# Second half of a hybrid block: queries, two mixtures of experts and attention in one program of numbered steps

## Chip, core, metric

One core of one Trainium2 chip runs the program. The metric is the device time of one launch in microseconds, as a median of several runs. Everything is computed in float32 precision. Engines are named as the profile names them: PE (TensorE), DVE (VectorE), ACT (ScalarE), POOL (GpSimd), SP (SyncE, which only issues transfers here).

## What is computed

The input x has 4 batches of 512 tokens of 128 numbers (16 tiles of 128 tokens). Cut to what matters:

```python
x = x + attn_a(layernorm(x))   # two test-time-training steps, then the queries through the trained weights
x = x + ffn(layernorm(x))      # mixture of experts
x = x + attn_b(layernorm(x))   # block-causal attention, 16 heads of 64, over 512 tokens
x = x + ffn(layernorm(x))      # the same mixture again
# attn_a ends:  h = swish(q @ gate) * (q @ val);  o = h @ proj @ proj_w + proj_b
# ffn:  gates = softmax(x @ Wg + bg);  the best 2 of 8, scaled to sum 1
#       out = sum over the chosen two of (x @ We[e] + be[e]) * gate
```

All 8 experts are computed for every token, and six of the eight weights are zero.

## The kernel before

The program has phases, each a block of its own with a barrier of all engines behind it. Up to the queries (projections, two rounds of gradients and of orthogonalisation) nothing changes but the table of biases below.

*Products.* A product that needs float32 precision is three matmuls (`mm3`, L100 to L102): both operands are split in a high part and the rest, and the rests' product is left out.

*Queries* (`query_phase`). Per batch of 512 tokens, four chunks of hidden units: two `mm3` (gate into q_G_, value into q_U_), sigmoid on ACT (L860), two products on DVE (L913, L919). Four output tiles of a batch (L890, 128x128 matmuls against the folded weight) stand between the chunks of the next. DVE adds them to x (L924) and takes statistics (L160).

*Mixture* (`moe_phase`, called twice). For all 16 tiles at once: mean and variance from the statistics (`ln_vector`, seven small DVE operations, a square root on ACT, a reciprocal). Per batch DVE normalises four tiles (L1095), PE transposes them (L1047), ACT and DVE split them (L1025, L1101), PE computes the scores of the experts (twelve matmuls with 8 columns). When all scores are there, one chain of small DVE operations on 128x128 values (L1112 to L1134) finds the two best experts of every token and their weights. PE turns the weights and multiplies them with a table that has the experts' biases at the places of all 16 tiles, and DVE adds that to x (L1140). Then, tile by tile, PE computes eight experts into two banks of PSUM; ACT scales three of them (L1037), POOL adds these up (L1014, L1016), DVE scales and adds the other five (L1158), POOL adds the two sums into x (L1005).

*Attention* (`attention_phase`). 32 pairs of heads, in each three groups of query tiles (tile 3; tile 2; tiles 1 and 0), so 96 steps. In step s PE computes the scores of group s, transposes the weights of group s-3, and projects the next queries (first step of a pair), keys (second) or values (third); in every third step it also multiplies a whole pair's weights with the values (L1409). DVE takes scores with mask and row minimum (L1484), copies transposed weights, keys, values (L1495, L1471, L1476), ACT does exponentials (L1325) and other copies, POOL scales rows (L1295). A step of the first group is called heavy below: it holds L1409's forty records; the steps of the second and third group are light. Eight banks of PSUM: three for scores (`psS`), two for transposed weights (`psT`), one for outputs of the heads (`psO`), two that projections and outputs take in turn (`psP`): a use waits until the use two places earlier is read.

Each engine runs its instructions in the order written in its loop and waits for semaphores of the others.

## Time and profile before

| | |
|---|---|
| median of 3 runs | 867.99 us (867.47 to 868.44) |
| the profiled execution's own time | 866.14 us |
| its span in the profile | 863.7 us |
| PE busy | 774.2 us (90%) |
| DVE busy | 545.4 us (63%) |
| ACT busy | 394.9 us (46%) |
| POOL busy | 270.7 us (31%) |
| chip clock granted to PE, mean | 0.94 |

The span is that of the profiled execution from its first to its last instruction; its own time includes 2.4 us around it. Busy times of engines overlap. PE runs at one of two clocks, 1.2 or 2.4 GHz; a granted clock of 0.50 in a stretch is the lower one. In timelines a row's "x6" merges six records of a kind; a 128x128 float32 matmul that isn't a transpose leaves two records, so L1419's 32 matmuls are x64.

### The profile page before, as it was taken

How to read it: one execution, taken by the hardware profiler on the slowest of the kernel's cores; microseconds unless marked ns; L12 is line 12 of the kernel's file. 1: busy time of each engine (PE TensorE's matmuls, PEld its weight loads, DVE VectorE, ACT ScalarE, POOL GpSimd, SP SyncE). 2: the span in 40 equal slices, each digit the busy share in tenths (PEclk: the TensorE clock that was granted, in tenths of full speed). 3: DMA queues.
4: the chain of work that ended last, by engine and by line, in shares of the span. 5: the costliest groups of instructions: out<-in, count | busy, mean ns of one | idle time of the engine just before them, and what ended most of it. 6: DMA issues, size and time to landing. Idle time of an engine off the chain costs nothing. (4 is left out here: it accounts for less than half of the span.)

```text
span 863.7 us, 15529 instructions
## 1 busy us (share of the span) xinstructions
PE 774.2 (90%) x5512; PEld 616.6 (71%) x5512; DVE 545.4 (63%) x1649; ACT 394.9 (46%) x1118; POOL 270.7 (31%) x476
## 2 busy tenths in 40 slices
PE   3669999897999988987858999999999999999786
PEld 1239999775999976677645677777777777777765
DVE  3945656444555535664796776776677666665468
ACT  4733333243333234312255766565556555564224
POOL 4830000002445002100372444343334333333027
PEclk9969999997999999895898999999999999999678
DMA  3040000000000000000000000000000000000001
GB/s 104 1 134 1 1 2 1 1 1 1 1 1 2 1 1 1 0 1 1 0 2 0 2 2 2 2 2 1 2 2 1 2 2 2 2 1 2 1 0 50
DMA packets 9466, 7.17 MB, mean 8 GB/s; under 512 B 1584, under 2 KB 9008, under 8 KB 9264
## 3 DMA queue, kind: packets, MB, share of 16 engines
q1 hardware_dynamic: 9392, 6.19, 2.3%
...
q14 instruction: 28, 0.23, 0.1%
...
## 5 line engine op out<-in xcount | busy, mean ns | idle before, releaser
L1295 POOL TENSOR_SCALAR t_p_<-t_p_,t_rinv_ 128x128 f32<-128x128 f32 (+3 forms) x256 | 132.1, 532 | 202.3 <-DVE t_rinv_ L1491 202.3
L1325 ACT ACTIVATE t_p_<-t_p_,t_nmin_ 128x128 f32<-128x128 f32 (+3 forms) x256 | 140.0, 551 | 9.1 <-DVE t_nmin_ L1484 9.1
L1484 DVE CUSTOM_DVE_ANT_0 t_p_<-t_S_,t_mask_ 128x128 f32<-128x128 f32 (+3 forms) x256 | 112.8, 487 | 21.7 <-PE t_S_ L1382 17.3
L1330 ACT ACTIVATE t_pT_<-t_T_ 128x384 f32<-128x384 f32 (+1 forms) x96 | 50.5, 526 | 118.3 <-PE t_T_ L1394 118.3
L1394 PEld LDWEIGHTS t_T_<-ident,t_p_ 128*128 128x128 f32 x640 | 68.2, 141 | 44.9 <-issue 26.0
L1382 PE MATMUL t_S_<-t_k_,t_q_ 64*128 64x256 f32 (+3 forms) x512 | 95.0, 468 | 0.1
L1394 PE MATMUL t_T_<-ident,t_p_ 128*128 128x128 f32 x640 | 90.8, 281 | 0.3 <-ACT t_pT_ L1330 0.3
L1409 PEld LDWEIGHTS t_O_<-t_pT_,t_v_ 128*64 128x64 f32 x1280 | 69.2, 137 | 11.0 <-ACT t_pT_ L1330 10.5
L1409 PE MATMUL t_O_<-t_pT_,t_v_ 128*64 128x128 f32 x1280 | 76.9, 275 | 0.0
L522 DVE SCALAR_TENSOR_TENSOR g_sw<-g_th,g_G 128x512 f32<-128x512 f32 x32 | 22.0, 688 | 71.3 <-ACT g_slope L436 66.2
L1382 PEld LDWEIGHTS t_S_<-t_k_,t_q_ 64*128 64x128 f32 x512 | 41.5, 185 | 26.9 <-DVE t_nmin_ L1484 12.3
L1495 DVE COPY t_pT_<-t_T_ 128x384 f32<-128x384 f32 (+1 forms) x96 | 57.3, 597 | 1.4 <-PE t_T_ L1394 1.3
L408 POOL TENSOR_TENSOR g_kl<-qkT,g_kh 128x128 fp32r<-128x128 f32 x32 | 14.6, 457 | 138.0 <-ACT g_kh L427 138.0
L1500 DVE COPY t_oT_<-t_O_ 128x512 f32<-128x512 f32 x32 | 22.1, 691 | 54.8 <-PE t_O_ L1409 54.8
L1325 ACT ACTIVATION_READ_ACCUMULATOR t_p_<-t_p_,t_nmin_ 128x1 f32 x256 | 48.6, 190 | 0.0
L440 ACT ACTIVATE g_hT<-g_H 128x512 f32<-128x512 f32 x32 | 19.1, 597 | 60.0 <-PE g_H L472 60.0
L1037 ACT ACTIVATE m_y_<-m_A_,m_wt_ 128x128 f32<-128x128 f32 x96 | 28.0, 367 | 25.4 <-PE m_A_ L102 25.4
L646 POOL TENSOR_TENSOR gvl<-gv,gvh 128x512 fp32r<-128x512 f32 x4 | 5.0, 1273 | 104.3 <-ACT gvh L751 104.3
L479 PEld LDWEIGHTS g_PT<-proj,g_hT 128*128 128x128 f32 x256 | 33.8, 193 | 2.6
L498 PE MATMUL acc<-qkv,g_dg 128*128 128x128 f32 x256 | 34.0, 276 | 1.0 <-DVE g_dg L549 1.0
L479 PE MATMUL g_PT<-proj,g_hT 128*128 128x128 f32 x256 | 34.1, 276 | 0.0
L498 PE MATMUL acc<-qkv,g_du 128*128 128x128 f32 x256 | 33.8, 275 | 0.0
(259 smaller groups left out, 1794.5 us busy)
## 6 DMA issues: line engine op xcount, KB each, us to landing
...
```

What stands on the lines that cost most here:

```text
L479: last = pe.matmul(pred, hT[:, t.ring, n * P:n * P + P], self.proj[:, n, :], start=(n == 0), stop=(n == NC - 1))
L498: last = pe.matmul(self.acc[:, n, m, :], src[:, t.ring, m * P:m * P + P], d[:, t.ring, :] if n == 2 else k, start=False, stop=False, skip_ ...
L1037: last = act.activation(y[:, t % 4, tile_of(k)], experts_of(t, e), ACT.Copy, scale=weight(t, e))
L1295: last = pool.tensor_scalar(pr[:, G.par, h, cols], pr[:, G.par, h, cols], rinv[:, G.par, n:n + 1], 1.0, ALU.mult, ALU.mult)
L1325: act.activation(pr[:, G.par, h, cols], pr[:, G.par, h, cols], ACT.Exp, bias=nmin[:, G.par, n:n + 1], scale=-1.0, accum_out=rsum[:, G.par, ...
L1330: act.activation(pT[:, G.par, 0, G.blocks], psT[:, 0, 0:G.width], ACT.Copy).then_inc(t["eA"], 1)
L1382: last = pe.matmul(psS[:, (2 * G.n + h) % 3, at_:at_ + (qt + 1) * P], qp[d, G.par, qt * P:qt * P + P], kp[d, G.par, 0:(qt + 1) * P], start ...
L1394: last = pe.transpose(psT[:, h, k:k + P], pr[:, G.par, h, at_:at_ + P], ident[:, :])
L1409: last = pe.matmul(psO[d, qt * P:qt * P + P], v[:, G.b % 2, n, G.p * P + h * DH:G.p * P + h * DH + DH], pT[:, G.par, h, at_:at_ + P], star ...
L1484: dve.tensor_tensor_reduce(pr[:, G.par, h, cols], psS[:, (2 * G.n + h) % 3, at_:at_ + keys], mask[:, SEQ - keys:SEQ], 1.0, -NEG, ALU.add, ...
L1495: dve.tensor_copy(pT[:, G.par, 1, G.blocks], psT[:, 1, 0:G.width]).then_inc(t["eB"], 1)
L1500: dve.tensor_copy(oT[:, b % 2, p, :], psO[:, :]).then_inc(t["oT"], 1)
```

## The change

Queries, both mixtures and the attention become one block, `second_half_phase`, without barriers. Its steps run from -38 to 116, and the attention's groups are steps 0 to 95 as before.

- The queries have steps -36 to -5, a chunk every second step, and the sixteen output products of a batch stand together in one step (-27, -19, -11, -3), in a bank of the scores.
- The two mixtures are eight *jobs*, one per batch: jobs 0 to 3 are the first mixture, 4 to 7 the second. `FRONT` is the step of a job's statistics; normalising, transposing, scores, top, three parts of the choice, weights and biases follow at +1 to +9. `EXPERTS` is the step of its first tile of experts; in the attention a tile's upper four experts (ACT scales all four, POOL sums) stand in one step and the lower four (DVE) in the next. Each job's chain works on 128x32 values instead of all tokens' 128x128.
- The standard deviation's inverse comes from a power of -0.5 on POOL, in place of ACT's root and DVE's reciprocal.
- psP has three banks, and the pair's outputs share them (`psO` is gone), as do all stages of the jobs: a use waits for the use three places earlier. Ten halves of tiles of jobs 6 and 7 use the five banks of scores and transposed weights once the attention is through with them.
- Each attention output tile is made in two halves of four heads' pairs. The last batch's first halves stand in steps 89 to 92, the second halves in step 101, with job 6's first experts.
- The biases' table has 32 rows instead of 128 and 512 columns instead of 2048, loaded by 4 transfers instead of 16.

```diff
-    LATE_LOADS = 10 + NT
+    LATE_LOADS = 10 + TPB
...
+    class Job:
+
+
+        FRONT = (-25, -17, 2, 20, 34, 58, 82, 102)
+        EXPERTS = (-16, -6, 11, 29, 43, 67, 101, 105)
...
+        def upper(self, n):
+
+            if self.closing == 1:
+                return self.first if n < 3 else self.front + 9
+            if self.closing == 0:
+                return self.first + (0, 1, 2, 4)[n]
+            return self.first + (n if self.j < 2 else 2 * n)
+
...
+        def summed(self, n):
+
+            if self.closing == 1:
+                return self.front + 9 + n
+            if self.closing == 0:
+                return self.first + (2, 3, 3, 5)[n]
+            return self.lower(n)
+
...
+            psG, psU, psO = psS[:, 0:2, :], psT, psS[:, 2, :]
...
+            QUERY = -36
+            ANSWER = 9
...
+            X_STEPS = [-9] + [IN_BATCH * b + 12 for b in range(BATCH - 1)]
+            OUT_STEPS = [IN_BATCH * b + step for b in range(BATCH)
+                         for step in (17, 18, 19, 20) + ((29, 30, 31, 32) if b < BATCH - 1 else (29, 29, 29, 29))]
...
+            halves = [("eh", 0), ("el", 0), ("eh", 1), ("el", 1), ("eh", 2)]
+            free = [psS[:, 0, :], psS[:, 1, :], psS[:, 2, :], psT[:, 0, :], psT[:, 1, :]]
+            spare = {(kind, j * TPB + n): bank_ for j in (NJ - 2, NJ - 1) for (kind, n), bank_ in zip(halves, free)}
...
+            emptied = {"q": (t["qe"], 1), "k": (t["ke"], 1), "v": (t["ve"], 1), "o": (t["res"], 1), "x": (t["xa"], 1),
+                       "pv": (t["oT"], 1), "mt": (m["l"], 1), "ml": (m["lg"], 1), "mw": (m["wl"], 1), "mb": (m["xb"], 1),
+                       "eh": (m["y"], 1), "el": (m["s"], 4)}
 
             def bank(kind, n):
-                return psP[:, place[kind, n] % 2, :]
+                return spare[kind, n] if (kind, n) in spare else psP[:, place[kind, n] % 3, :]
 
             def wait_bank(e, kind, n):
 
+                if (kind, n - TPB) in spare:
+                    sem, times = emptied[kind]
+                    e.wait_ge(sem, (n - TPB + 1) * times)
+                    return
+                if (kind, n) in spare:
+                    e.wait_ge(t["mx"], 8 * self.PAIRS)
+                    e.wait_ge(t["eA"], N)
+                    e.wait_ge(t["eB"], N)
+                    return
                 at_ = place[kind, n]
-                if at_ >= 2:
-                    before, m = uses[at_ - 2]
-                    e.wait_ge(emptied[before], m + 1)
+                if at_ >= 3:
+                    kind_, n_ = uses[at_ - 3]
+                    sem, times = emptied[kind_]
+                    e.wait_ge(sem, (n_ + 1) * times)
...
+                def power(kind, n, b):
+                    pool.wait_ge(t["var"], norm_of[kind, n] + 1)
+                    rows = slice(b * TPB, b * TPB + TPB)
+                    pool.tensor_tensor(self.rstd[:, rows], self.lnw[:, 3, rows], self.mhalf[:, rows], ALU.pow).then_inc(t["root"], 1)
+
+                def add_experts(J, n):
+                    i = J.j * TPB + n
+                    pool.wait_ge(m["y"], i + 1)
+                    if i:
+                        pool.wait_ge(m["z"], i)
+                    pool.tensor_tensor(half[:, :, :], y[:, i % 2, 0:2, :], y[:, i % 2, 2:4, :], ALU.add).then_inc(m["z0"], 1)
+                    pool.wait_ge(m["z0"], i + 1)
+                    if i > 1:
+                        pool.wait_ge(m["s"], 4 * (i - 2) + 2)
+                    pool.tensor_tensor(z[:, i % 2, :], half[:, 0, :], half[:, 1, :], ALU.add).then_inc(m["z"], 1)
+
+                def close(J, n):
+                    i = J.j * TPB + n
+                    pool.wait_ge(m["s"], 4 * i + 4)
+                    pool.tensor_tensor(x[:, J.b * TPB + n, :], a[:, i % 2, :], b_[:, i % 2, :], ALU.add).then_inc(m["x"], 1)
...
+                def output(b, half, n):
+                    i = (2 * b + half) * TPB + n
                     wait_bank(pe, "o", i)
-                    pe.wait_ge(t["oT"], (b + 1) * NP)
-                    for n in range(NP):
-                        last = pe.matmul(bank("o", i)[:, 0:P], oT[:, b % 2, n, m * P:m * P + P], wout[:, n, :],
-                                         start=(n == 0), stop=(n == NP - 1))
+                    pe.wait_ge(t["oT"], b * NP + half * TPB + TPB)
+                    for p in range(half * TPB, half * TPB + TPB):
...
+                def experts(J, n, kind, first, done):
+                    i = J.j * TPB + n
+                    cols = slice(first, first + 512)
+                    wait_bank(pe, kind, i)
+                    mm3(pe, bank(kind, i), mh[:, J.par, tile_of(n)], ml[:, J.par, tile_of(n)], weh[:, cols], wel[:, cols]).then_inc(done, 1)
...
+                for s in STEPS:
                     G, T, O = at(s, 0), at(s, LT), at(s, LV)
+                    if s == QUERY - 1:
+                        fold()
                     if G:
                         scores(G)
                     if T:
                         turn(T)
-                    if G:
...
+                def moments(b):
+                    st, rows = self.stats[:, b * TPB:b * TPB + TPB, :], slice(b * TPB, b * TPB + TPB)
+                    w = self.lnw[:, :, rows]
+                    taken.wait()
+                    chain(dve.tensor_tensor(w[:, 0, :], st[:, :, 1], st[:, :, 4], ALU.subtract))
+                    chain(dve.tensor_tensor(w[:, 1, :], w[:, 0, :], w[:, 0, :], ALU.mult))
+                    chain(dve.tensor_tensor(w[:, 2, :], st[:, :, 2], st[:, :, 5], ALU.add))
+                    chain(dve.scalar_tensor_tensor(w[:, 3, :], w[:, 1, :], P / 4.0, w[:, 2, :], ALU.mult, ALU.add))
...
+                def rank(J, src, high_, chosen):
+
+                    e_ = eq[:, J.par, :, :]
+                    g, h, k = src[:, J.par, :, :], high_[:, J.par, :], pm[:, J.par, :]
+                    link.next(dve.tensor_reduce(h, g, AX.X, ALU.max))
+                    link.wait()
+                    link.next(dve.tensor_tensor(e_, g, wide(h), ALU.is_equal))
+                    link.wait()
+                    link.next(dve.tensor_tensor(e_, e_, prio[:, :, :], ALU.mult))
+                    link.wait()
+                    link.next(dve.tensor_reduce(k, e_, AX.X, ALU.max))
+                    link.wait()
+                    link.next(dve.tensor_tensor(chosen[:, J.par, :, :], e_, wide(k), ALU.is_equal))
+
+                def route(J, part):
+                    r = J.par
+                    if part == 0:
+                        dve.wait_ge(m["prio"], 1)
+                        dve.wait_ge(m["e"], J.j + 1)
+                        link.wait()
+                        rank(J, gate, top1, sel)
+                    if part == 1:
+                        link.wait()
+                        link.next(dve.scalar_tensor_tensor(gate2[:, r, :, :], sel[:, r, :, :], -2.0, gate[:, r, :, :], ALU.mult, ALU.add))
+                        link.wait()
+                        rank(J, gate2, top2, sel2)
+                    if part == 2:
+                        link.wait()
+                        link.next(dve.tensor_tensor(tot[:, r, :], top1[:, r, :], top2[:, r, :], ALU.add))
+                        link.next(dve.tensor_tensor(sel[:, r, :, :], sel[:, r, :, :], sel2[:, r, :, :], ALU.add))
+                        link.wait()
+                        link.next(dve.tensor_tensor(sel[:, r, :, :], sel[:, r, :, :], gate[:, r, :, :], ALU.mult))
+                        link.next(dve.reciprocal(rtot[:, r, :], tot[:, r, :]))
+                        link.wait()
+                        dve.tensor_tensor(wt[:, r, :, :], sel[:, r, :, :], wide(rtot[:, r, :]), ALU.mult).then_inc(m["c"], 1)
+
...
+                def accumulate(J, n):
+                    i = J.j * TPB + n
+                    weight = lambda e: wt[:, J.par, n, e:e + 1]
+                    dve.wait_ge(m["c"], J.j + 1)
+                    dve.wait_ge(m["xb"], J.j + 1)
+                    dve.wait_ge(m["E"], i + 1)
+                    if i > 1:
+                        dve.wait_ge(m["x"], i - 1)
+                    for e in range(4):
+                        acc = (a, b_)[e % 2][:, i % 2, :]
+                        if e == 1:
+                            dve.wait_ge(m["z"], i + 1)
+                        if e > 1:
+                            dve.wait_ge(m["s"], 4 * i + e - 1)
+                        so_far = (x[:, J.b * TPB + n, :], z[:, i % 2, :])[e] if e < 2 else acc
+                        dve.scalar_tensor_tensor(acc, bank("el", i)[:, tile_of(e)], weight(e), so_far,
+                                                 ALU.mult, ALU.add).then_inc(m["s"], 1)
+
...
                     k.schulz_phase(step)
-            k.query_phase()
-        k.moe_phase(0)
-        k.attention_phase()
-        k.moe_phase(1)
+        k.second_half_phase()
```

Three places of the order show the moves. The first is on PE: the end of the queries before, and then a piece of the changed queries, from the third step with output products (m_A_ and t_P_ are banks that mixtures and projections use, q_O_ and t_S_ take the queries' outputs, t_T_ now also takes the value products).

```order
L100 MATMUL q_U_<-q_qh_,gvh 128x512
L101 MATMUL q_U_<-q_ql_,gvh 128x512
L102 MATMUL q_U_<-q_qh_,gvl 128x512
L890 MATMUL q_O_<-q_pw_,q_hT_ 128x128 x20
L829 UNCONDITIONAL_BRANCH
L1040 UNCONDITIONAL_BRANCH
L1047 MATMUL m_A_<-ident,m_xn_ 128x128 x8
L100 MATMUL m_A_<-wgh,m_xh_ 128x8
L101 MATMUL m_A_<-wgl,m_xh_ 128x8
```

```order
L1233 MATMUL t_S_<-t_pw_,t_oT_ 128x128 x16
L115 MATMUL t_S_<-t_xh_,gvh 128x512
L116 MATMUL t_S_<-t_xl_,gvh 128x512
L117 MATMUL t_S_<-t_xh_,gvl 128x512
L115 MATMUL t_T_<-t_xh_,gvh 128x512
L116 MATMUL t_T_<-t_xl_,gvh 128x512
L117 MATMUL t_T_<-t_xh_,gvl 128x512
L1331 MATMUL t_P_<-ident,t_mwt_ 32x128
L115 MATMUL t_S_<-t_xh_,gvh 128x512
L116 MATMUL t_S_<-t_xl_,gvh 128x512
L117 MATMUL t_S_<-t_xh_,gvl 128x512
L115 MATMUL t_P_<-beh,t_wTh_ 128x512
```

Before, the transposes and scores of a mixture stand behind the queries and a barrier; now a job's turned weights and its bias product stand between a query's chunks.

The second is on DVE in the attention: a second step of a pair before, and the end of step 34 in the change (lnw is the layer normalisation's scratch, t_k_ the keys, t_a_ and t_b_ a tile's sums).

```order
L1484 ISA t_p_,t_nmin_<-t_S_,t_mask_ 128x384
L1484 ISA t_nmin_ 128x1
L1484 ISA t_p_,t_nmin_<-t_S_,t_mask_ 128x384
L1484 ISA t_nmin_ 128x1
L1495 COPY t_pT_<-t_T_ 128x384
L1491 RECIPROCAL t_rinv_<-t_rsum_ 128x2
L1471 COPY t_k_<-t_P_ 128x512
L1484 ISA t_p_,t_nmin_<-t_S_,t_mask_ 128x256
L1484 ISA t_nmin_ 128x1
L1484 ISA t_p_,t_nmin_<-t_S_,t_mask_ 128x128
L1484 ISA t_nmin_ 128x1
```

```order
L1395 TENSOR_TENSOR lnw<-stats 128x4
L1396 SCALAR_TENSOR_TENSOR lnw<-lnw 128x4
L1397 TENSOR_SCALAR lnw<-lnw 128x4
L1398 TENSOR_TENSOR lnw<-stats 128x4
L1399 TENSOR_SCALAR mean<-lnw 128x4
L1420 COPY t_k_<-t_P_ 128x512
L1578 SCALAR_TENSOR_TENSOR t_a_<-t_P_,t_mwt_,x 128x128
L1578 SCALAR_TENSOR_TENSOR t_b_<-t_P_,t_mwt_,t_z_ 128x128
L1578 SCALAR_TENSOR_TENSOR t_a_<-t_P_,t_mwt_,t_a_ 128x128
L1578 SCALAR_TENSOR_TENSOR t_b_<-t_P_,t_mwt_,t_b_ 128x128
L1433 ISA t_p_,t_nmin_<-t_S_,t_mask_ 128x256
L1433 ISA t_nmin_ 128x1
```

Before, the row minima of the next group follow the keys' copy at once; in step 34 two layer normalisations (fourteen operations), two statistics and four expert sums stand between.

The third is on PE where the attention ends.

```order
L1409 MATMUL t_O_<-t_pT_,t_v_ 64x128 x20
L1394 MATMUL t_T_<-ident,t_p_ 128x128 x12
L1409 MATMUL t_O_<-t_pT_,t_v_ 64x128 x20
L1419 MATMUL t_P_<-wout,t_oT_ 128x128 x32
L1214 UNCONDITIONAL_BRANCH
L1040 UNCONDITIONAL_BRANCH
L1047 MATMUL m_A_<-ident,m_xn_ 128x128 x8
L100 MATMUL m_A_<-wgh,m_xh_ 128x8
L101 MATMUL m_A_<-wgl,m_xh_ 128x8
```

```order
L1283 MATMUL t_T_<-ident,t_p_ 128x128 x14
L1299 MATMUL t_P_<-t_pT_,t_v_ 64x128 x20
L1283 MATMUL t_T_<-ident,t_p_ 128x128 x12
L1299 MATMUL t_P_<-t_pT_,t_v_ 64x128 x20
L1309 MATMUL t_P_<-wout,t_oT_ 128x128 x16
L115 MATMUL t_S_<-weh,t_mh_ 128x512
L116 MATMUL t_S_<-wel,t_mh_ 128x512
L117 MATMUL t_S_<-weh,t_ml_ 128x512
L115 MATMUL t_S_<-weh,t_mh_ 128x512
```

Before, 32 output matmuls end the phase and the mixture starts behind a barrier with transposes; now sixteen remain, and job 6's experts follow at once in banks of the scores.

## Rows read from the trace of the kernel before

**Rows 1.** Busy time by stretch: PE, PEld, DVE, ACT, POOL, PE clock, DMA share, GB/s.

```profile
342.80:462.60 119.80, 94.64 (x427) 76.44 (x427) 78.98 (x221) 37.95 (x85) 29.90 (x65) 0.81 0.00 1
462.60:796.70 334.10, 333.63 (x2907) 244.59 (x2906) 239.39 (x834) 208.40 (x645) 135.84 (x259) 1.00 0.01 2
796.70:863.70 67.00, 51.16 (x237) 42.85 (x237) 41.83 (x142) 19.66 (x57) 21.74 (x56) 0.78 0.06 16
```

**Rows 2.** Timeline at phase seams: start, us, engine, line, operation, idle before it.

```profile
345.97 0.79 PE L100 MATMUL q_G_<-q_qh_,gvh 128*128 128x512 f32 x1 [1.40 <-DVE q_ql_ L907]
...
386.50 5.44 PE L890 MATMUL q_O_<-q_pw_,q_hT_ 128*128 128x128 f32 x32 [1.89 <-DVE x L924]
...
452.90 1.12 PE L1351 MATMUL t_P_<-ident,t_xn_ 128*128 128x128 f32 x4 [8.69 <-DVE t_xn_ L1461]
...
809.39 2.14 PE L1047 MATMUL m_A_<-ident,m_xn_ 128*128 128x128 f32 x8 [4.47 <-DVE m_xn_ L1095]
```

**Rows 3.** Timeline of one pair of heads and the next one's start, PE and DVE.

```profile
535.07 1.13 PE L1382 MATMUL t_S_<-t_k_,t_q_ 64*128 64x512 f32 x4
...
540.17 0.92 PE L1382 MATMUL t_S_<-t_k_,t_q_ 64*128 64x384 f32 x4
540.29 0.69 DVE L1500 COPY t_oT_<-t_O_ 128x512 f32<-128x512 f32 x1 [2.07 <-PE t_O_ L1409]
...
543.82 0.28 DVE L1484 CUSTOM_DVE_ANT_0 t_p_<-t_S_,t_mask_ 128x128 f32<-128x128 f32 x1
...
544.88 1.13 PE L1382 MATMUL t_S_<-t_k_,t_q_ 64*128 64x512 f32 x4
```

**Rows 4.** Timeline: tight expert matmuls, cold logits, output matmuls, small DVE operations.

```profile
427.37 0.39 PE L102 MATMUL m_A_<-weh,m_xl_ 128*128 128x512 f32 x1
427.60 0.39 PE L100 MATMUL m_A_<-weh,m_xh_ 128*128 128x512 f32 x1
...
410.19 0.35 PE L101 MATMUL m_A_<-wgl,m_xh_ 128*128 128x8 f32 x1
...
410.41 0.35 PE L102 MATMUL m_A_<-wgh,m_xl_ 128*128 128x8 f32 x1
...
797.54 7.38 PE L1419 MATMUL t_P_<-wout,t_oT_ 128*128 128x128 f32 x64 [0.89 <-DVE t_oT_ L1500]
...
806.55 0.17 DVE L167 TENSOR_TENSOR lnw<-lnw 128x16 f32<-128x16 f32 x1
806.76 0.19 DVE L168 TENSOR_TENSOR lnw<-stats 128x16 f32<-128x16 f32 x1
...
827.54 0.29 DVE L1122 TENSOR_TENSOR m_eq_<-m_gate_,m_m_ 128x128 f32<-128x128 f32 x1
```

**Rows 5.** Groups of lines: busy, mean ns of one, idle before.

```profile
L1037 ACT ACTIVATE m_y_<-m_A_,m_wt_ 128x128 f32<-128x128 f32 x96 | 28.0, 367 | 25.4 <-PE m_A_ L102 25.4
...
L160 DVE BATCH_NORM_STATS2 stats<-x 128x6 f32<-128x128 f32 x64 | 15.2, 276 | 5.1 <-DMA x<-in_L_attn_a_x_dram 5.0
...
L1014 POOL TENSOR_TENSOR m_z_<-m_y_ 128x128 f32<-128x128 f32 x32 | 14.7, 460 | 50.7 <-ACT m_y_ L1037 50.7
...
L913 DVE TENSOR_TENSOR q_sw_<-q_G_,q_sg_ 128x512 f32<-128x512 f32 x16 | 11.0, 689 | 11.6 <-ACT q_sg_ L860 11.6
L1158 DVE SCALAR_TENSOR_TENSOR m_b_<-m_A_,m_wt_,m_z_ 128x128 f32<-128x128 f32 x32 | 10.9, 340 | 1.9 <-POOL m_z_ L1016 1.0
...
L1095 DVE TENSOR_SCALAR m_xn_<-x,mean,rstd 128x128 f32<-128x128 f32 x32 | 8.7, 339 | 0.1
```

**Rows 6.** Tile q_ql_ written on DVE from two operands in SBUF: minimum, median, maximum.

```profile
L907 DVE TENSOR_TENSOR q_ql_<-qkT,q_qh_ x4: 672/881/1766, 344.8 to 367.5; 128x512 fp32r<-128x512 f32 x4
```

**Rows 7.** Busy time in two microseconds each, columns as in the first group.

```profile
28.00:30.00 2.00, 1.47 (x7) 0.58 (x5) 2.00 (x7) 1.82 (x8) 1.84 (x3) 1.00 0.01 4
388.00:390.00 2.00, 2.00 (x11) 2.00 (x11) 0.00 (x0) 0.00 (x0) 0.00 (x0) 0.50 0.00 0
```

**Rows 8.** Timeline of the last addition.

```profile
860.51 0.45 POOL L1005 TENSOR_TENSOR x<-m_a_,m_b_ 128x128 f32<-128x128 f32 x1 [0.69 <-DVE m_b_ L1158]
```

861 lines of the change are left out of this document (416 added, 445 removed).

## Prediction

> **What bounds the kernel now.** I cut the busy times at three seams, because the change leaves everything ahead of 342.8 us alone [rows 1]. What the reader should see: from the first scores to the last copied head output, 334.1 us, PE is busy 333.6 at the full clock, so this stretch lasts as long as PE's own work. The 119.8 us ahead of it and the 67.0 behind it are another matter: PE is busy 94.6 and 51.2 us there, and at a mean granted clock of 0.81 and 0.78. The timeline at the seams says why [rows 2]: PE waits 1.89 us for the add of the queries, 8.69 before the attention, 4.47 before the second mixture, for DVE each time, and the matmul that follows takes longer than at full clock (the queries' first 0.79 us, against 0.39 for the same shape in rows 4). So there are 187 us in which neither engine is full, and 334 in which PE is.
>
> Within the attention I looked at one pair of heads [rows 3]. The heavy step takes 5.10 us (535.07 to 540.17), the two light ones 4.71 together (to 544.88). DVE is idle 2.07 us in the heavy one, waiting for PE's head outputs. In the light ones it is nearly full: the first minimum of the third group ends at 544.10 and PE's next scores start at 544.88, so DVE may be some 0.8 us late before PE notices.
>
> **What the change costs and saves.** Work hardly changes; it moves. From the seams, three parts.
>
> *A, up to the first scores (119.8 us now).* From the block's start to the first gate product 3.2 us, as now. Then PE's and DVE's work is chained: a batch's answer (its output products) needs its last hidden product, and DVE's next work needs the answer. One answer is 32 records, 3.7 us by the 0.115 us a record of the output projection [rows 4], 5.4 when it starts cold [rows 2]; with idle before each I take 5. Up to the first answer nine steps of one `mm3` each, the first few cold: 10 us. Between the answers DVE sets the time; by mean durations [rows 5] and 0.21 us for each chained small operation [rows 4], 0.24 on 128x32 values (between 0.21 at 16 columns and 0.29 plus issue at 128):
> - before answer 1: add 0.7, six gate products 4.1, statistics 1.1, moments 1.5, normalise 1.4, two splits 1.4, scores and top 0.7, together 10.9; in between waits for transposes, ACT and twelve cold score matmuls at 0.22 [rows 4], 3: 14.
> - before answer 2: the same kinds, the choice's third part 1.1, weights and bias 1.0, seven gate products 4.8 and the four tiles of job 0 (16 sums of 0.34, 5.4): 20, and 3 for ACT's and POOL's sums: 23.
> - before answer 3: 14 of DVE, 3 of waits, 3 of PE's projections and experts: 20.
>
> 10 + 14 + 23 + 20, four answers 20, and 3.2: **90 us**, so 30 less. ACT's four changes of table between sigmoid and exponential lie in its idle time. The power on POOL has no row: below it is a small operation of DVE (0.2 [rows 4]), above it twice POOL's addition on 32 times the values (0.46 [rows 5]), 0.9; I take 0.3, nearest to the small one, in four places: it decides 2 us at most. Bounds of A: 63 (PE's 60 us at the full clock) and 110 (PE at the lower clock through most of it).
>
> *B, the attention (334.1 us).* PE is full here, so what is added counts whole. Four more half outputs move in: 4 x 8 x 0.115 = 3.7. Jobs 2 to 5 bring 32 `mm3` of experts: three intervals of 0.23 [rows 4] and 0.08 for a changed operand are 0.77: 24.6. Jobs 2 to 6 bring transposes and turned weights (0.6), twelve scores (half of the cold 0.22, since the clock is full: 1.3) and a bias `mm3` (0.77), 2.7 each: 13.4. Then DVE's light steps. Of its added work what stands in a pair's second step is lost beyond 0.8 us: step 34 has two statistics, fourteen layer-normalisation operations and four sums, 4.8, less 0.8 and PE's own 0.7: 3.3; step 58 2.1, step 10 1.0, steps 40, 64 and 88 (part of the choice, 1.4) 0.6 each, steps 7 and 25 0.4 each, others 1: 10. What stands in the third or first step falls into the 2.07 us of idle time (normalising, the bias, half of the sums); if that cover were gone, each job would cost 3 to 4 us more. 334.1 + 3.7 + 24.6 + 13.4 + 10 = **386 us**, 52 more. ACT has room (208 of 334) for 16 scalings of 0.37 a job. Bounds: 376 without loss, 405 with every added DVE operation lost that doesn't meet a longer PE step. The third bank stands in for the head outputs' own; uses three back are read within a step, so I cost that at nothing. Its cover is DVE being less than a step late.
>
> *C, from the last head output (67.0 us).* Copy 0.7, sixteen output matmuls 3.7, add and statistics 0.8, moments 1.1, power 0.3, normalise 1.4, transposes and splits 2.3, scores cold 2.6, take and top 0.7, exponential 0.3; then DVE stands behind job 6's last tile (ACT's four scalings 1.5, two sums on POOL [rows 5] 1.2, three on DVE 1.1) 3.8; sixteen operations of the choice 3.8, weights 1.0, bias 2.0, four tiles of four sums 5.4 and one wait 1.0; last addition to the end 3.2 [rows 8]. Sum **34 us**, 33 less. Experts of jobs 6 and 7 lie beside it on PE.
>
> 342.8 + 90 + 386 + 34 = 852.8 against 863.7: 11 us less. The profiled execution took 866.14, the median is 867.99, 1.85 above, so 857 us. The smaller biases' table leaves POOL's two long operations in the second gradient round shorter, beside work of PE: nothing.
>
> **A rule on the port.** The tile q_ql_, two operands in SBUF, took 0.67 us alone and 1.77 at 344.8, when POOL added the projection's bias [rows 6]. The change puts some seventeen small operations of a job with two such operands beside POOL's scaling (135.8 us busy in 334 [rows 1]). If a third of them wait 0.3 us, a job has 1.7 us more, half of it in light steps: some 4 us, in a rival below. By the Trainium skill, SBUF — State Buffer, "Who interferes with whom", a DVE instruction with two SBUF inputs contends with a GpSimd instruction that reads SBUF, and whichever is second waits; the trace agrees in this one tile.
>
> **Rivals.**
> 1. *DVE takes over in the attention: slower.* For: in light steps it has 0.8 us, and each job adds some 15 us to it. If each step takes as long as its busier engine, without help from neighbours, my lists give 23 us of loss instead of 10, and the port 4 more: 386 + 17 = 403, total **874**. Against: the heavy step's 2.07 us return with every pair. It decides from 20 us of loss on. Chance 0.2.
> 2. *The lower clock stays.* For: after 1.89 us of idleness PE ran at half for its answer [rows 2, 7], and part A has such gaps ahead of all four. If it stays low, answers take 8 and experts double: A 108, total **875**. Against: at 28 us PE worked 1.47 of 2 us and kept the full clock [rows 7]. By the Trainium skill, TensorE: Matmul & The Clock Gate, "A second HAM failure mode", short idling between groups of matmuls while cycling through PSUM banks can throw the clock back and forth; rows 1 show 1.00 through the attention with two banks in turn, so here the trace disagrees. Chance 0.07.
> 3. *Overlap is better than I think: faster.* Waits in A fall to 80 us and DVE's losses in B to 2: total **839**. For: my waits are added one behind another, though steps of two engines slide. Chance 0.25.
> 4. *Nothing gained:* B costs what A and C give, 397: total 868. Chance 0.05.
>
> **Numbers.** My forecast holds 0.43 (850 to 865), nearly all of it faster. About 0.2% (1.7 us) is what a measurement of this kernel tells from no change. Faster: 0.43 + 0.25 + a little of rival 4 = 0.69; same 0.06; slower 0.25 (rivals 1, 2). The range 834 to 878 reaches over rivals 1 and 3 to their middles and a little beyond; likeliest alone 848 to 866.
>
> **What would show it.** First scores near 433 us (90 behind 342.8); last head output near 819; end 34 later. PE busy in the attention above 96% at clock 1.00, with its idle time put down to DVE and sitting in steps 34 and 58; one answer about 5 us. Small DVE operations at 0.2 us say that the port is free; at 0.4 rival 1 grows. Wrong: first scores after 445 (clock or chain), B over 397, or C over 40, which would mean that the choice's chain or the last tile's sums hold more than I list.

## Result and profile after

The changed kernel takes 874.13 us (median of 8 runs, 871.97 to 876.35), the kernel before 866.79 beside it (864.66 to 868.44): 1.0082 of it, 95% interval 1.0063 to 1.0101. It is slower by 0.8% where I forecast 857, faster. The profiled execution took 874.45 us, its span 872.7.

First the same three stretches as in [rows 1], cut where the first scores and the last copy of head outputs now stand (columns as there).

```profile
342.60:434.30 91.70, 74.67 (x342) 58.20 (x342) 58.63 (x172) 32.85 (x68) 24.48 (x44) 0.85 0.00 1
434.30:834.70 400.40, 378.06 (x3135) 280.49 (x3134) 309.57 (x1116) 232.12 (x724) 170.79 (x315) 1.00 0.01 3
834.70:872.70 38.00, 23.89 (x100) 18.33 (x100) 19.84 (x74) 9.76 (x35) 13.98 (x25) 0.77 0.05 14
```

| | before | forecast | after |
|---|---|---|---|
| A, to the first scores | 119.8 | 90 | 91.7 |
| B, attention | 334.1 | 386 | 400.4 |
| PE busy in B | 333.6 | 376 | 378.1 |
| PE idle in B | 0.5 | 10 | 22.3 |
| C, to the end | 67.0 | 34 | 38.0 |

A gave what it should. The miss is 14 us of B and 4 of C, and 12 of B's 14 are idle time of PE. What PE waited for in B (the waits of that stretch, longest in total first; each line has who waited, the releaser behind the arrow, us in total, times, and the longest):

```profile
PE t_P_ L1299 <- ACT t_q_ L1147: 7.1, 5, 2.0
PE t_S_ L1271 <- DVE t_nmin_ L1433: 7.0, 8, 2.4
...
PE t_P_ L1241 <- DVE t_v_ L1425: 2.3, 1, 2.3
...
PE t_P_ L115 <- ACT t_q_ L1147: 1.5, 1, 1.5
PE t_P_ L115 <- DVE t_k_ L1420: 1.5, 1, 1.5
...
PE t_P_ L1317 <- DVE t_v_ L1425: 0.9, 1, 0.9
PE t_P_ L115 <- DVE t_wTl_ L1556: 0.9, 1, 0.9
```

Two kinds of wait stand here. 7.1 + 1.5 = 8.6 us end when **ACT** has read the queries: the bank of the head outputs (L1299), or of an expert tile (L115), was last given to them. The rest ends with **DVE**, but for 0.7 us that end with ACT's copies of transposed weights near the end of B. Neither the first kind nor its place was in my sum. One of the six, in the timeline around step 42:

```profile
607.42 1.15 POOL L1073 TENSOR_SCALAR t_p_<-t_p_,t_rinv_ 128x384 f32<-128x384 f32 x2 [2.45 <-DVE t_rinv_ L1440]
...
608.10 0.51 DVE L1547 TENSOR_TENSOR t_msel_<-t_msel_ 128x32 f32<-128x32 f32 x1
...
608.49 0.48 PE L115 MATMUL t_P_<-t_xh_,wh 128*128 128x512 f32 x1
...
609.07 0.68 DVE L1433 CUSTOM_DVE_ANT_0 t_p_<-t_S_,t_mask_ 128x512 f32<-128x512 f32 x1
...
609.27 1.05 PE L1309 MATMUL t_P_<-wout,t_oT_ 128*128 128x128 f32 x8
...
609.79 0.72 ACT L1152 ACTIVATE t_p_<-t_p_,t_nmin_ 128x512 f32<-128x512 f32 x1 [0.87 <-DVE t_nmin_ L1433]
...
610.16 0.27 PE L1331 MATMUL t_P_<-ident,t_mwt_ 128*32 128x128 f32 x1
...
610.51 0.71 ACT L1152 ACTIVATE t_p_<-t_p_,t_nmin_ 128x512 f32<-128x512 f32 x1
...
611.22 0.57 ACT L1147 ACTIVATE t_q_<-t_P_ 128x512 f32<-128x512 f32 x1
...
611.85 0.88 PE L1299 MATMUL t_P_<-t_pT_,t_v_ 128*64 128x128 f32 x12 [1.42 <-ACT t_q_ L1147]
```

PE has the queries ready at about 609.4 and the turned weights at 610.4, then stands 1.42 us. ACT reads the queries (L1147) at 611.22 only, behind two exponentials, which wait for DVE's row minima. In its queue the read stands behind work that comes through DVE. In the first two rows L1547 (two operands in SBUF) takes 0.51 us where it takes 0.18 on the mean with POOL hardly at work (run short_scaling below), and it ends at 608.61, when POOL's two records end (608.57).

The second kind is densest in steps 34 to 36:

```profile
571.32 1.36 POOL L1073 TENSOR_SCALAR t_p_<-t_p_,t_rinv_ 128x512 f32<-128x512 f32 x2 [1.76 <-DVE t_rinv_ L1440]
...
571.44 0.58 DVE L1393 TENSOR_TENSOR lnw<-stats 128x4 f32<-128x4 f32 x1
...
572.06 0.63 DVE L1394 TENSOR_TENSOR lnw<-lnw 128x4 f32<-128x4 f32 x1
...
572.72 0.17 DVE L1395 TENSOR_TENSOR lnw<-stats 128x4 f32<-128x4 f32 x1
...
575.66 0.50 PE L115 MATMUL t_P_<-weh,t_mh_ 128*128 128x512 f32 x1 [1.50 <-DVE t_k_ L1420]
...
577.34 1.13 PE L1271 MATMUL t_S_<-t_k_,t_q_ 64*128 64x512 f32 x4 [0.71 <-DVE t_nmin_ L1433]
...
578.21 3.61 DVE L1404 TENSOR_SCALAR qkT<-x,mean,rstd 128x128 f32<-128x128 f32 x8
...
582.47 0.66 PE L1241 MATMUL t_P_<-ident,qkT 128*128 128x128 f32 x4 [2.29 <-DVE t_v_ L1425]
...
585.11 0.65 PE L115 MATMUL t_P_<-weh,t_mh_ 128*128 128x512 f32 x1 [1.55 <-ACT t_q_ L1147]
...
585.57 0.63 PE L116 MATMUL t_P_<-wel,t_mh_ 128*128 128x512 f32 x1
```

Fourteen moments of two layer normalisations and then eight normalisings of 128x128 hold DVE's copies back, and PE stands 1.50, 0.71, 2.29 and 1.55 us. L1393 and L1394 end at 572.02 and 572.69, where the first and the second of POOL's two scalings end (half and all of 1.36 us from 571.32): 0.58 and 0.63 us for operations that take 0.16. After that PE runs at the slower clock for a while: between 585.3 and 588.7 the granted clock is 0.50 (L116 0.63 us against 0.39).

Behind the attention, the last job's choice stands behind the sums of job 6's last tile:

```profile
849.53 0.79 PE L115 MATMUL t_P_<-weh,t_mh_ 128*128 128x512 f32 x1 [0.73 <-DVE t_b_ L1578]
...
849.82 0.23 DVE L1516 TENSOR_TENSOR t_mlogit_<-t_mlogit_,t_mtop_ 128x32 f32<-128x32 f32 x1
...
850.12 0.63 PE L116 MATMUL t_P_<-wel,t_mh_ 128*128 128x512 f32 x1
...
855.94 0.35 DVE L1578 SCALAR_TENSOR_TENSOR t_a_<-t_P_,t_mwt_,x 128x128 f32<-128x128 f32 x1 [5.89 <-PE t_P_ L117]
...
856.99 0.18 DVE L1522 TENSOR_REDUCE t_mtop_<-t_mgate_ 128x4 f32<-128x32 f32 x1
...
860.31 0.19 DVE L1552 TENSOR_TENSOR t_mwt_<-t_msel_,t_mrtot_ 128x32 f32<-128x32 f32 x1
...
860.65 0.27 PE L1331 MATMUL t_P_<-ident,t_mwt_ 128*32 128x128 f32 x1 [3.51 <-DVE t_mwt_ L1552]
```

L1516 is done at 850.05, but DVE's next instruction waits 5.89 us for an expert product that PE issues behind the upper experts of three tiles of job 7, part of it at a clock of 0.50 (L116 takes 0.63 us). The choice starts at 856.99.

### The profile page after: what moved, and what is told of

Read it like the earlier page. It is cut to its first block, busy times and chain, and to the rows that moved or that the text cites. A ratio compares the mean times of both kernels' runs of the same rounds, so it can differ in the third digit from the quotient of the medians.

```text
span 872.7 us, 15873 instructions
## 1 busy us (share of the span) xinstructions
PE 771.4 (88%) x5518; PEld 609.6 (70%) x5518; DVE 573.0 (66%) x1813; ACT 403.9 (46%) x1158; POOL 284.9 (33%) x481
## 4 chain that ended last, share of the span: by engine, by line
PE 39%; DVE 11%; issue 5%; POOL 2%; ACT 2%; POOLq 0%; DVEq 0%; ACTq 0%
PE t_S_ L1271 8%; PE t_P_ L1299 8%; PE t_T_ L1283 7%; PE t_P_ L115 4%; PE t_P_ L117 3%; PE t_P_ L116 3%; DVE t_p_ L1433 3%; PE t_P_ L1309 2%; PE t_S_ L1233 2%; DVE qkT L1404 1%; ACT t_p_ L1152 1%; DVE t_pT_ L1444 1%; POOL t_half_ L1088 1%; POOL t_z_ L1092 1%; DVE t_v_ L1425 1%
## 5 line engine op out<-in xcount | busy, mean ns | idle before, releaser
L1073 POOL TENSOR_SCALAR t_p_<-t_p_,t_rinv_ 128x128 f32<-128x128 f32 (+3 forms) x256 | 133.4, 537 | 213.6 <-DVE t_rinv_ L1440 212.9
L1299 PE MATMUL t_P_<-t_pT_,t_v_ 128*64 128x128 f32 x1280 | 78.0, 277 | 7.1 <-ACT t_q_ L1147 7.1
L1299 PEld LDWEIGHTS t_P_<-t_pT_,t_v_ 128*64 128x64 f32 x1280 | 70.3, 138 | 17.4 <-ACT t_q_ L1147 9.3
L1449 DVE COPY t_oT_<-t_P_ 128x512 f32<-128x512 f32 x32 | 22.0, 689 | 43.7 <-PE t_P_ L1299 43.7
L1182 ACT ACTIVATE t_y_<-t_P_,t_mwt_ 128x128 f32<-128x128 f32 x104 | 29.6, 367 | 19.7 <-issue 14.3
L1088 POOL TENSOR_TENSOR t_half_<-t_y_ 128x256 f32<-128x256 f32 x32 | 23.4, 733 | 36.7 <-ACT t_y_ L1182 24.7
L1309 PEld LDWEIGHTS t_P_<-wout,t_oT_ 128*128 128x128 f32 x256 | 32.8, 191 | 3.4 <-DVE t_oT_ L1449 1.1
```

What stands on the lines that cost most here:

```text
L1073: last = pool.tensor_scalar(pr[:, G.par, h, cols], pr[:, G.par, h, cols], rinv[:, G.par, n:n + 1], 1.0, ALU.mult, ALU.mult)
L1299: last = pe.matmul(bank("pv", pair)[d, tile_of(qt)], v[:, (2 * b + p // TPB) % 3, n, p % TPB * P + h * DH:p % TPB * P + h * DH + DH], pT[: ...
L1309: last = pe.matmul(bank("o", i)[:, 0:P], oT[:, p, tile_of(n)], wout[:, p, :], start=(p % TPB == 0), stop=(p % TPB == TPB - 1))
```

## Experiments

Three theories on B. **1, places:** PE waits because a bank's reader stands late in its own engine's queue (ACT's read of the queries), and because much DVE work stands in one light step. **2, amount:** DVE has too much work in all (rival 1), wherever it stands. **3, port:** DVE's operations with two operands in SBUF are held up by POOL. B and C are taken from the profiled execution of each run (first scores, last copy of head outputs); B repeats best: with next to nothing in it changed it was 400.3, 400.3 and 400.4 us, while the time ahead of the queries' first product, which no edit touches, lay between 343.9 and 348.1 us in the profiled executions. The medians of the kernel before, taken beside each set of runs, lie between 865.6 and 866.8 us, so whole times are best compared by the ratio.

| run | median us (runs) | of before, 95% | B | PE idle in B | C |
|---|---|---|---|---|---|
| the change | 874.13 (8) | 1.0082 (1.0063 to 1.0101) | 400.4 | 22.3 | 38.0 |
| q_first | 866.58 (12) | 0.9998 (0.9982 to 1.0015) | 392.3 | 14.5 | 37.2 |
| own_bank | 895.58 (5) | 1.0336 (1.0315 to 1.0356) | 413.4 | 26.8 | 40.4 |
| x_later | 870.61 (6) | 1.0049 (1.0037 to 1.0060) | 395.5 | 17.3 | 37.3 |
| takes_first | 875.99 (4) | 1.0116 (1.0098 to 1.0133) | 400.6 | 20.0 | 38.0 |
| job_later | 867.56 (12) | 1.0012 (0.9996 to 1.0029) | 392.8 | 13.8 | 38.0 |
| tail_acc | 871.35 (6) | 1.0071 (1.0046 to 1.0095) | 400.3 | 22.3 | 34.3 |
| pow_cheap | 871.85 (6) | 1.0081 (1.0055 to 1.0107) | 400.3 | 22.3 | 36.2 |
| short_scaling | 864.85 (12) | 0.9991 (0.9977 to 1.0004) | 391.0 | 13.3 | 37.7 |
| short_choice | 869.89 (6) | 1.0053 (1.0035 to 1.0071) | 397.7 | 17.8 | 36.0 |
| three | 860.75 (9) | 0.9948 (0.9931 to 0.9966) | 389.8 | 11.5 | 34.4 |
| three_bias | 859.66 (6) | 0.9927 (0.9909 to 0.9944) | 389.0 | 11.1 | 33.2 |
| apart | 855.72 (5) | 0.9883 (0.9863 to 0.9903) | 385.3 | 9.4 | 33.4 |

**q_first: ACT's read of the queries.**

```diff
+                    for pair in planned(Q_STEPS, s):
+                        if s >= 0:
+                            take_q(pair)
                     if G:
                         exps(G)
...
                     for pair in planned(Q_STEPS, s):
-                        take_q(pair)
+                        if s < 0:
+                            take_q(pair)
```

> ACT copies the next queries out of their bank (L1147) before the step's exponentials instead of behind them; nothing else changes. Theory 1, the ring of three banks: in steps 12, 36, 42, 60, 66 and 90 PE stands 1.13, 1.55, 1.42, 1.98, 1.41 and 1.12 us, together 8.6, because the bank that the heads' outputs (once an expert tile) want was last given to that step's queries, and ACT reads these behind two exponentials. Then these waits go, and the attention is 6 to 8 us shorter (400 to about 393, total about 867). Theory 2, DVE is what the attention is waiting for: PE then waits for DVE's row minima in the same places, and the total changes by less than 2 us.

B fell by 8.1 us, PE's idle time by 7.9. The place of one read in ACT's queue was half of the miss in B. The same spot in its timeline (lines here stand four lower in the code):

```profile
604.37 0.48 PE L115 MATMUL t_P_<-t_xh_,wh 128*128 128x512 f32 x1
...
605.15 1.05 PE L1313 MATMUL t_P_<-wout,t_oT_ 128*128 128x128 f32 x8
605.35 0.60 ACT L1147 ACTIVATE t_q_<-t_P_ 128x512 f32<-128x512 f32 x1 [0.54 <-PE t_P_ L117]
...
605.85 0.71 ACT L1152 ACTIVATE t_p_<-t_p_,t_nmin_ 128x512 f32<-128x512 f32 x1
...
606.04 0.27 PE L1335 MATMUL t_P_<-ident,t_mwt_ 128*32 128x128 f32 x1
...
606.25 2.40 PE L1303 MATMUL t_P_<-t_pT_,t_v_ 128*64 128x128 f32 x40
```

The read now waits 0.54 us for PE and not for the exponentials, and the head outputs follow at once. None of PE's waits in B ends with the queries any more; in step 36 one of 1.03 us for another of ACT's copies (the normalised input) came in their place, and the one for the values fell there from 2.29 to 0.69 us. Theory 2 said under 2 us: it doesn't explain this part.

**own_bank: head outputs as before, the rest on two banks.**

```diff
-            psS, psT, psP = ps("S", [P, 3, 512]), ps("T", [P, 2, 512]), ps("P", [P, 3, 512])
+            psS, psT, psP = ps("S", [P, 3, 512]), ps("T", [P, 2, 512]), ps("P", [P, 2, 512])
+            psV = ps("V", [P, 512])
...
+                if kind == "pv":
+                    if n:
+                        e.wait_ge(t["oT"], n)
+                    return
                 at_ = place[kind, n]
-                if at_ >= 3:
-                    kind_, n_ = uses[at_ - 3]
+                if at_ >= 2:
+                    kind_, n_ = uses[at_ - 2]
```

> The heads' outputs have a bank of their own again, as before the change, and all other uses (projections, output tiles, jobs) take two banks in turn. Theory 1: the waits of the heads' outputs for ACT's queries go, but now a use waits for the one two places back, and 22 uses of the attention meet one of their own step, eight of them the queries that ACT reads late; I expect those 8 to wait 1 to 2 us each and the others 0.3 to 0.5: 5 to 15 us slower than the changed kernel. Theory 2 (DVE sets the pace, the banks don't matter): within 2 us of the changed kernel.

B is 13 us longer, as expected of theory 1, and the whole 21, which is more: A and C use the same ring and lost 5 and 2.5. The waits of the head outputs (L1299) are gone, and the eight uses that now stand two behind their own step's queries wait 0.55 to 1.96 us, 9.5 in all. In B only 4.5 us more are idle time; PE is busy 8.5 us more for the same 3,135 matmuls, and the mean granted clock is 0.98 where it was 1.00. So more waiting can go with a loss beyond its own length.

```profile
439.40:852.70 413.30, 386.49 (x3135) 284.92 (x3134) 309.85 (x1115) 232.39 (x724) 170.18 (x315) 0.98 0.01 3
```

**x_later: the attention's layer normalisation one step later.**

```diff
-            X_STEPS = [-9] + [IN_BATCH * b + 12 for b in range(BATCH - 1)]
+            X_STEPS = [-9] + [IN_BATCH * b + 13 for b in range(BATCH - 1)]
```

> The attention's layer normalisations of batches 1 to 3 stand one step later (transposes in steps 13, 37, 61), so that the two of steps 34 to 36 and 58 to 60 are a step apart and the normalising of one falls into the heavy step. Theory 1: PE stood 6.0 us in steps 34 to 36 and 5.3 in 58 to 60, with 1.7 more for a slower clock at 585 us, because fourteen moments and then eight normalisings stand in one step ahead of DVE's copies; apart, half of that goes, and the heads' outputs of step 12 and 60 no longer meet their own queries' bank: 5 to 8 us less in total. Theory 2: DVE's work over these three steps is the same sum, so at most 3 us less.

4.9 us in B, 3.5 in the medians (2.9 by the ratios): short of the 5 to 8 of theory 1, and in the whole time not clear of theory 2's 3. Of the 5.0 us of PE's idle time that went, 3.4 are waits for ACT's queries (steps 12 and 60), as one use fewer stands between those queries and the head outputs there. The pile in steps 35 and 59 shrank, but the values' projection two steps on now waits for the split of the input (0.72 and 1.23 us in steps 14 and 62).

**takes_first: DVE's copies ahead of its layer normalisation.** takes(s) holds the calls of take_k, take_v and add_output.

```diff
+                    if s >= 0:
+                        takes(s)
                     for b in planned(X_STEPS, s + 2):
                         moments(b)
...
                     for J in jobs(s, NORM):
                         norm(J)
-                    for pair in planned(K_STEPS, s):
-                        take_k(pair)
...
+                    if s < 0:
+                        takes(s)
```

> In the attention DVE copies keys and values out of their banks and adds the output tiles (L1420, L1425, L1457) before the step's moments and normalising instead of behind them. Theory 1: PE's waits of 1.50, 2.29 and 0.91 us that end with these copies (at 575.7, 582.5 and 686.8 us) go; the ones for the row minima and for ACT's queries stay: 3 to 5 us less. Theory 2: DVE is late by its whole work, so the wait moves on to the row minima or to the normalised rows: less than 1 us.

Nothing gained, and my theory 1 was wrong here: the waits for keys and values went, and the ones for the row minima, the normalised rows and the queries grew (1.87 us at step 35, where 1.50 and 0.71 had stood). PE's idle time fell by 2.3 us, and its busy time grew by 2.5 at a mean granted clock of 0.987 in B, where it was 0.996. So B itself says nothing for either theory; the waits say that inside one step DVE was late by most of its work, as theory 2 says: those that end with DVE in steps 34 to 36 are 3.3 us where they were 4.5, and theory 1 wanted 3.8 of these 4.5 gone.

**job_later: jobs 4 to 6 one step later.**

```diff
-        FRONT = (-25, -17, 2, 20, 34, 58, 82, 102)
+        FRONT = (-25, -17, 2, 20, 35, 59, 83, 102)
```

> The fronts of jobs 4, 5 and 6 (moments, normalising, transposes, scores, choice) stand one step later (35, 59, 83 instead of 34, 58, 82), the experts where they are; the attention's own layer normalisations stay in steps 34 to 36 and 58 to 60. Theory 1, DVE is late where light steps are piled up, and the place decides, not the amount: a job's normalising now falls into the heavy step, where DVE idles 2 us; PE's idle time in steps 34 to 36 falls from 6.0 to about 3, in 58 to 60 from 5.3 to about 3, in 83 from 1.14 to 0.4, and the slow clock at 585 us may not come: 5 to 7 us less in total. Theory 2, the amount decides: 0 to 2 us less.

B 7.6 us shorter, with the same work on DVE (309.1 us busy, 309.6 in the change). Theory 2 said 0 to 2. But the edit moves more than DVE's work: the jobs' banks move too, and so what stands ahead of the head outputs in the ring.

```profile
PE t_P_ L1299 <- ACT t_q_ L1147: 2.4, 2, 1.3
```

PE's waits for ACT's queries fell from 8.6 us to these 2.4 (those of steps 42, 60, 66 and 90 are gone), all its other waits by 2.4 only. So most of this gain is of the kind that q_first shows. What is left for DVE's work itself is what job_later adds behind q_first in the run three: 2.5 us. That much is the place of the work: a normalising in a heavy step lies in idle time of DVE.

**tail_acc: the last choice ahead of the last tile.**

```diff
-                return self.first + (2, 3, 3, 5)[n]
+                return self.first + (2, 3, 3, 9)[n]
```

> DVE's four sums of job 6's last tile stand behind the last job's choice (step 110) instead of ahead of it (106). In the changed kernel DVE stands 5.9 us for that tile's expert product, which PE issues behind three of job 7's at the slower clock, and the choice starts at 857.0 instead of about 850. Theory: the weights are then ready near 853.5 and PE's queue of experts, done at 857, becomes the limit: 3 to 4 us less. Rival: the waits behind (bias, job 7's tiles, POOL) are what ends last, and what the choice gains is lost there: under 1 us.

C 3.7 us shorter, B the same; the medians differ by 2.8, the ratios by 0.0011, whose intervals overlap. The weights are ready at 855.7, and PE turns them at 858.4, behind its experts.

**pow_cheap: a product for the power.**

```diff
-  pool.tensor_tensor(self.rstd[:, rows], self.lnw[:, 3, rows], self.mhalf[:, rows], ALU.pow)
+  pool.tensor_tensor(self.rstd[:, rows], self.lnw[:, 3, rows], self.mhalf[:, rows], ALU.mult)
```

> POOL multiplies by -0.5 where it took the power of -0.5, so the normalised values are other numbers; the work is the same otherwise. The power takes 1.02 us, where I had taken 0.3. If the rest of the chain is as I think, the small product takes 0.1 to 0.3 and gives back 0.8 us in each chain that PE waits for: two or three places ahead of the attention, one behind it, and up to four in it: 3 to 5 us less in total. Rival: the chains are hidden behind the queries and attention and only the last job gains: about 1 us.

```profile
L1081 POOL TENSOR_TENSOR rstd<-lnw,mhalf x9: 198/200/202, 441.5 to 840.6; 128x4 f32<-128x4 f32 x9
```

0.20 us in place of 1.02. C fell by 1.7 us, of which 0.8 is this operation and the rest goes with a shorter stretch at the slower clock (mean 0.83 against 0.77). B didn't move, nor did A: from the queries' first product to the first scores it takes 88.2 us against 88.4. Only the last job gains, as the rival said. The medians differ by 2.3 us, the ratios hardly (1.0081 and 1.0082), so the whole time shows no gain clear of noise.

**short_scaling: POOL out of the way.**

```diff
+                        cols = slice(cols.start, cols.start + 16)
                         last = pool.tensor_scalar(pr[:, G.par, h, cols], ...)
```

> POOL scales 16 columns of each block of the attention's weights where it scaled 128 to 512, so most weights stay unscaled and POOL is nearly idle in the attention. Theory 3, the port: in the changed kernel DVE's operations with both operands in SBUF take longer while POOL works (L1396 0.46 us against 0.16, L1404 0.51 against 0.34, L1416 1.42 against 0.67, L1549 0.41 against 0.19), some 15 us of DVE's time in the attention, and about a third of that stands where PE waits for DVE. Then PE's idle time in the attention falls from 22 to about 17 us, and the attention from 400 to 395. If the stretch lies beside PE's work: the operations get shorter, the attention stays at 399 to 400.

B fell by 9.4 us, nearly twice what I expected, and PE's idle time by 9. Groups of lines on DVE in B, of the change:

```profile
L1404 DVE TENSOR_SCALAR qkT<-x,mean,rstd 128x128 f32<-128x128 f32 x32 | 12.7, 465 | 0.0
...
L1416 DVE TENSOR_TENSOR t_xl_<-qkT,t_xh_ 128x512 fp32r<-128x512 f32 x3 | 4.2, 1415 | 6.1 <-ACT t_xh_ L1143 6.1
...
L1396 DVE SCALAR_TENSOR_TENSOR lnw<-lnw 128x4 f32<-128x4 f32 x8 | 3.1, 383 | 0.3
L1526 DVE TENSOR_TENSOR t_meq_<-t_meq_,t_prio_ 128x32 f32<-128x32 f32 x10 | 2.9, 290 | 0.3
```

and of short_scaling (lines one lower in the code):

```profile
L1405 DVE TENSOR_SCALAR qkT<-x,mean,rstd 128x128 f32<-128x128 f32 x32 | 9.2, 353 | 0.0
...
L1417 DVE TENSOR_TENSOR t_xl_<-qkT,t_xh_ 128x512 fp32r<-128x512 f32 x3 | 2.4, 805 | 6.1 <-ACT t_xh_ L1144 6.1
...
L1527 DVE TENSOR_TENSOR t_meq_<-t_meq_,t_prio_ 128x32 f32<-128x32 f32 x10 | 1.9, 192 | 0.3
...
L1397 DVE SCALAR_TENSOR_TENSOR lnw<-lnw 128x4 f32<-128x4 f32 x8 | 1.3, 162 | 0.3
```

DVE is busy 296.6 us against 309.6: 13 us of its time in the attention went with POOL's work, 3.5 of them in the normalising (L1404, one tensor and two scalars a partition) and nearly all the others in operations with two tensors in SBUF; operations that read PSUM kept their times. In B of the change, 32 of the small ones (128x4 and 128x32) took over 0.06 us more than their median in short_scaling, and each of these 32 ended within 0.04 us behind the end of one of POOL's scalings (L1073). The waits for ACT's queries shrank as well (8.6 to 6.3 us; 1.42 to 0.76 in step 42), because the exponentials in front of the queries come from DVE. No wait of PE in B of the change ended with POOL, so POOL's own shorter work can hold little of the gain directly.

**short_choice: the choice in two operations.**

```diff
+                    if J.j > 1:
+                        link.next(dve.tensor_tensor(chosen[:, J.par, :, :], g, wide(h), ALU.is_equal))
+                        return
                     link.next(dve.tensor_tensor(e_, g, wide(h), ALU.is_equal))
```

> Jobs 2 to 7 find an expert in two operations instead of five (the order among equal gates is left out): twelve to fourteen tenths of a microsecond of DVE less in each job, in its steps 5 to 6. Theory 1, only what stands in a step where DVE is late costs: these steps (25 and 26, 39 and 40, 63 and 64, 87 and 88) show no idle time of PE but 0.43 us here and there, so the attention gets under 1 us shorter; behind the attention, where the choice is on the path, 1.3 us. Theory 2, DVE's whole amount sets the attention's time: five jobs, 3 to 6 us less in the attention.

B 2.6 us shorter, above theory 1's limit and below theory 2's range; C 2.0. PE's idle time fell by 4.5 us, in step 60 by 1.2, in 42 and 66 by 0.7 each, where the wait for ACT (1.42, now 0.74) had been fed by a choice that ended late in the step ahead; the clock took 1.8 back (PE busy 379.9).

**three, three_bias, apart: put together.** three is q_first, job_later and tail_acc in one; three_bias adds

```diff
-                    for b in planned(X_STEPS, s):
+                    for b in planned(X_STEPS, s - 2):
                         add_bias(b)
```

and apart adds to that

```diff
-        FRONT = (-25, -17, 2, 20, 35, 59, 83, 102)
-        EXPERTS = (-16, -6, 11, 29, 43, 67, 101, 105)
+        FRONT = (-25, -17, 2, 20, 38, 62, 83, 102)
+        EXPERTS = (-16, -6, 11, 29, 46, 70, 101, 105)
```

> Queries read ahead of the exponentials (as in q_first), fronts of jobs 4 to 6 one step later, and the last tile's sums behind the last choice, together. If they are independent the gains add up: 7.3 measured for the first, 4 to 6 for the second (without the slow clock's part where the first took it already) and 3.5 for the third: 857 to 861, faster than the kernel before by 0.7 to 1 per cent. If DVE sets the pace in the attention (theory 2), the first two overlap: 864.

> The three changes of the run called three, and POOL adds the output bias two steps later, so that DVE's split of the attention's input (L1416, 1.42 us three times beside POOL's addition, 0.67 without) no longer meets it. By theory 3 DVE gets 0.7 us back in steps 12, 36 and 60, where PE waits for it or right behind: 0.5 to 1.5 us less than three, 859.5. If nobody waits for the split: the same as three.

> three_bias with jobs 4 and 5 three steps later (fronts 38 and 62 in place of 35 and 59, experts from 46 and 70), so that no layer normalisation of a job stands beside one of the attention. In three PE still stands 2.8 us in steps 35 and 36 and 2.4 in 59 and 60, for DVE each time, and steps 36 runs partly at the slower clock. Theory 1, coincidence costs: alone, each normalisation costs what the one of steps 9 to 11 does, 0.9 us (a job's in the heavy step 0.1): 2 to 4 us less than three_bias, about 856 to 858. Theory 2, the amount costs: no difference, 859.7.

```profile
434.50:820.00 385.50, 375.95 (x3135) 279.29 (x3134) 307.15 (x1116) 236.94 (x725) 170.33 (x315) 1.00 0.01 3
```

In B the first two gains overlap (10.6 us, not 8.1 + 7.6), because both take away waits for ACT's queries; the whole, 860.75, lies at the upper edge of the 857 to 861 that I expected of independent gains. three_bias gained 0.7 in B: DVE was busy 1.8 us less, which fits the port, but PE's waits in steps 36 and 60 stayed (1.85 and 1.20 us), and only some 0.4 us in steps 13 and 14 went. The medians' 1.1 alone would not show it. In apart PE stands in steps 35 and 36 for 1.4 us instead of 2.8, the slower clock there is gone (PE busy 375.9), and B is another 3.7 us shorter with the same work. Neither kernel has a wait for ACT's queries, so this gain is the place of DVE's work alone. It takes 0.9883 of the kernel before (0.9863 to 0.9903) and is the fastest of all, 2% below the change as it was.

## Why the prediction was wrong

**Right.** *A*: 90 forecast, 91.7 measured. Its terms were a little less right than their sum: the four answers took 3.81, 3.73, 5.44 and 3.73 us where I took 5 each, and the stretch ahead of the fourth took 24 us where I took 20; the three before it were within 1 us. The clock came back each time (mean 0.85), so rival 2 is out. What its text makes of [rows 1] was too much, though: PE idled 0.5 us in that attention, so its clock of 1.00 is no test of short idling. In the change, with waits, it fell to 0.50 at 585.3. *PE's work in B*: 376 forecast, 378.1 measured, of which some 1.7 are the slower clock in 585.3 to 588.7. What was moved costs what the rows before said.

**Wrong: "uses three back are read within a step, so I cost that at nothing. Its cover is DVE being less than a step late".** This is the step of the sum that failed, 8.6 of B's 14.4 us. Head outputs stand at the end of a heavy step, which begins with the next queries. Where two other uses (a job's, an output tile's, the attention's input) stand between them, the use three places back is the same step's queries: by the kernel's list of uses in steps 12, 18, 30, 42, 60, 66 and 90, and in 36 for an expert tile. Their reader is ACT, not DVE, behind two exponentials. PE stood in six of these eight, and q_first took these waits away. Before the change the head outputs had their own bank [rows 3] and nothing like it showed. I named a cover on the wrong engine and never wrote down which use stands three back of which. DVE still has a part in it, through the row minima that the exponentials wait for: with POOL out of the way 6.3 of the 8.6 us stayed.

**Mis-sized: DVE's losses, 10 us.** 22.3 less 8.6 is 13.7, of which 0.7 end with ACT's copies of transposed weights. By step: 34 to 36 cost 4.5 without the wait for ACT (I had 3.3), 58 to 60 3.4 (2.1), step 83 1.1 (in "others"), steps 10 and 11 0.9 (1.0), the first five steps 1.7 and three places of 0.43 (not listed). The choices' steps 40, 64 and 88 cost nothing themselves; their end was handed on to ACT's read (short_choice halved it in steps 42 and 66). What I left out of the forecast is the port. I saw it in [rows 6] and put 4 us for it into a rival. By short_scaling it is up to 9.4 us of B, through both kinds of wait (POOL's shorter work itself may hold a part of that). By the Trainium skill, SBUF — State Buffer, "Who interferes with whom", a DVE instruction with two SBUF inputs contends with a GpSimd instruction that reads SBUF, for ports that are locked for one of them; the rows agree (0.58 and 0.63 us, ending with POOL's scalings; PSUM operands at 0.34 unchanged). By the same section a tensor-by-scalar operation can hold the shared pair too, which L1404 shows: 0.47 us beside POOL, 0.35 without.

**Mis-sized: C.** "DVE stands behind job 6's last tile ... 3.8": with the exponential's 0.3 that is 4.1, and it took from 850.05 to 856.99, 6.9, because PE issues that tile's lower experts behind job 7's and mostly at half the clock; tail_acc shortened C by 3.7. The power was 1.02 where I took 0.3, and four normalisings, beside POOL again, took 2.15 where I took 1.4. Other terms were smaller, so C is 4 over and not 5.

**The whole.** By stretches the forecast was 20 us short, by the medians 17: I took the 4.3 us between span and median as before, and in the change they are 1.4. That is luck, not part of the reasoning.

**The rivals.** Rival 1 has the time (874), in part by luck (its B of 403 is 2.6 over, its A and C are 5.7 under, and the same 2.9 between span and median come off), and half of the mechanism: DVE is late and POOL stretches it, but the largest single part was a read on ACT, and moving the same DVE work takes some of the lateness away (2.5 us by one step, 3.7 by three more). Its rule, each step as long as its busier engine, holds in the main inside a step (takes_first) and not across steps (three, apart). Of its 27 us of loss 22.3 came. Rival 3 asked for 2 us of losses in B; the best version here still has 9.4. PE was busy 94.4% of B where I said above 96, and its waits stood not only in steps 34 and 58 but in heavy steps.

**What stays open.** Of the 9.4 us that are left in apart, 0.7 end with ACT's copies of transposed weights near the end of B, some 2.6 stand in the first six steps; the rest, some 6, ends with DVE. How it splits between the port and the amount wasn't tried.
